# Cross-attention kernel: a third buffer for the exponentials, and new issue orders for TensorE, ScalarE and VectorE

## The reference

```python
qn = _layer_norm(Q, ln_q_g, ln_q_b)
q = (qn @ Wq + bq).reshape(B, Lq, H, DH).transpose(0, 2, 1, 3)
k = (KV @ Wk + bk).reshape(B, Lkv, H, DH).transpose(0, 2, 1, 3)
v = (KV @ Wv + bv).reshape(B, Lkv, H, DH).transpose(0, 2, 1, 3)
scores = jnp.einsum('bhqd,bhkd->bhqk', q, k) / jnp.sqrt(jnp.float32(DH))
attn = jax.nn.softmax(scores, axis=-1)
ctx = jnp.einsum('bhqk,bhkd->bhqd', attn, v)
ctx = ctx.transpose(0, 2, 1, 3).reshape(B, Lq, D)
x = Q + (ctx @ Wo + bo)
h = _layer_norm(x, ln_ff_g, ln_ff_b)
ff = jax.nn.silu(h @ W1 + b1) @ W2 + b2
return x + ff
```

## Time and profile before

| | |
|---|---|
| median of 3 runs | 3438.5 us (3438.05 to 3440.09) |
| the profiled execution's own time | 3438.9 us |
| its span | 3437.1 us |
| TensorE busy | 3363.7 us, 98% |
| VectorE busy | 2505.0 us, 73% |
| ScalarE busy | 2240.1 us, 65% |
| GpSimd busy | 952.1 us, 28% |

### The profile page before, as it was taken

One profiled execution on the slowest core, in us unless ns is written; L12 is line 12 of the kernel. 1 busy time (PEld: TensorE's weight loads), 2 busy tenths in 40 slices (PEclk: granted clock), 3 DMA queues, 4 the chain that ended last, 5 costly groups with the idle time before them and its releaser, 6 DMA issues.

```text
span 3437.1 us, 52453 instructions
## 1 busy us (share of the span) xinstructions
PE 3363.7 (98%) x19620; PEld 1621.4 (47%) x19620; DVE 2505.0 (73%) x4613; ACT 2240.1 (65%) x2859; POOL 952.1 (28%) x1340
## 2 busy tenths in 40 slices
PE   6899999999999999999999999999999999999997
PEld 2334544444444445444445444444444455444435
DVE  5777777777777867777777777767777777777761
ACT  2566667666676666667666676666767666676663
POOL 5032324223332322324222232232314222242201
PEclk7999999999999999999999999999999999999998
DMA  4322212232122322212232122321223231122200
GB/s 103 64 42 44 51 33 55 45 71 42 35 48 36 71 45 43 50 37 57 45 69 38 32 54 38 70 45 35 51 39 61 45 64 36 35 55 43 45 7 13
DMA packets 121534, 162.95 MB, mean 47 GB/s; under 512 B 37040, under 2 KB 102592, under 8 KB 118208
## 3 DMA queue, kind: packets, MB, share of 16 engines
q1 hardware_dynamic: 120896, 159.40, 23.6%
q10 hardware_dynamic: 384, 0.20, 0.0%
HBM read 46.43 MB, written 8.39 MB: 16 GB/s over the span
## 4 chain that ended last, share of the span: by engine, by line
PE 95%; DVE 2%; ACT 1%; SPq 0%; DMA 0%; issue 0%; POOL 0%; ACTq 0%; DVEq 0%
PE o_ps L1241 23%; PE rows_ps L1207 22%; PE scores L1222 21%; PE side L1171 6%; PE side L1175 6%; PE side L1160 5%; PE side L1152 5%; DVE chunk_max L1006 2%; PE side L1156 2%; PE side L1164 2%; PE side L1143 1%; PE side L1146 0%; ACT probs L811 0%; PE scores L1171 0%; PE side L1167 0%; PE side L1150 0%
## 5 line engine op out<-in xcount | busy, mean ns | idle before, releaser
L1006 DVE TENSOR_REDUCE chunk_max<-rows_ps 128x1 f32<-128x512 f32 (+1 forms) x3328 | 2110.8, 666 | 778.7 <-PE rows_ps L1207 772.0
L811 ACT ACTIVATE probs<-scores 128x1024 f32<-128x1024 f32 (+1 forms) x1664 | 1653.4, 1022 | 727.8 <-PE scores L1222 559.7
L1207 PE MATMUL rows_ps<-k_stack,q_stack 96*128 96x512 bf16 (+1 forms) x4096 | 1139.5, 337 | 22.6 <-DVE chunk_max L1006 15.9
L1222 PE MATMUL scores<-q_stack,k_stack 99*128 99x512 bf16 (+1 forms) x3328 | 984.9, 379 | 5.0 <-ACT probs L811 3.0
L1241 PE MATMUL o_ps<-probs,v_sb 128*32 128x512 f32 x6656 | 850.2, 602 | 2.3 <-ACT probs L811 2.2
L1207 PEld LDWEIGHTS rows_ps<-k_stack,q_stack 96*128 96x128 bf16 x4096 | 338.3, 98 | 717.7 <-DVE chunk_max L1006 469.7
L1222 PEld LDWEIGHTS scores<-q_stack,k_stack 99*128 99x128 bf16 (+1 forms) x3328 | 320.0, 99 | 391.1 <-issue 94.5
L1241 PEld LDWEIGHTS o_ps<-probs,v_sb 128*32 128x32 f32 x6656 | 148.9, 108 | 359.8 <-issue 280.9
L648 POOL TENSOR_TENSOR o_sb<-o_sb,denom 128x512 f32<-128x512 f32 x32 | 40.6, 1268 | 896.5 <-DVE denom L992 896.5
L592 POOL TENSOR_TENSOR rest<-whole,k_parts 128x512 f32<-128x512 f32 x124 | 117.1, 944 | 548.7 <-ACT k_parts L776 541.8
L1175 PE MATMUL side<-w_sb,ffT 128*128 128x256 f32 x960 | 261.3, 381 | 0.0
(11 more groups left out here) (130 smaller groups left out, 2160.0 us busy)
## 6 DMA issues: line engine op xcount, KB each, us to landing
k_stack<-k_parts SPq DMA_DIRECT2D x768, 50.0 KB, 2.2
k_stack<-k_stack SPq DMA_DIRECT2D x192, 200.1 KB, 5.6
ctx_nat<-in_ctx SPq DMA_DIRECT2D x47, 512.0 KB, 4.0
q_stack<-q_stack SPq DMA_DIRECT2D x192, 64.0 KB, 3.4
q_stack<-q_parts SPq DMA_DIRECT2D x756, 16.0 KB, 1.8
x_nat<-in_x SPq DMA_DIRECT2D x16, 512.0 KB, 6.0
resid<-in_x SPq DMA_DIRECT2D x32, 256.0 KB, 2.8
out<-resid SPq DMA_DIRECT2D x32, 256.0 KB, 2.4
```

The source lines that it names most:

```text
L811: nc.scalar.activation(probs[0:rows, (q + t) % 2, 2 * LQ * pair:2 * LQ * (pair + 1)], scores[0:rows, 2 * LQ * pair:2 * LQ * (pair + 1)], A ...
L1006: nc.vector.tensor_reduce(dst, src, AX.X, ALU.max).then_inc(rows_read, 1)
L1207: last = nc.tensor.matmul(rows_ps[:, m % 2, d0:d0 + w], q_stack[s][0:STACK, h, P * t:P * (t + 1)], k_stack[s][0:STACK, h, k0:k0 + w], star ...
L1222: ins = nc.tensor.matmul(scores[0:keys_in(t), LQ * j:LQ * (j + 1)], k_stack[s][:, h, P * t:P * t + keys_in(t)], q_stack[s][:, h, :], start ...
```

## The change

`probs` gets three buffers instead of two; tile t of a quarter uses the buffer of its running number over the whole kernel, modulo 3, and the first `e` of a tile waits for the PV of the tile three before. The orders are made anew, with the same letters in the same numbers in every quarter of every string. In TENSOR letters `p` now stand together in twos and threes more often.

```diff
 QT = LQ // P
 HH = H // 2
 UNITS = KT * 2
+PROBS = 3
 PARTS = 3
 K_ROWS = (0, 0, 0, 1, 1, 2)
 Q_ROWS = (0, 1, 2, 0, 1, 0)
...
 
 
 TENSOR = (
-    "pmddsssmmsddddddmssmpmdsssdmdsmddsdddmmpssmmsddmdmdssspmmsddddmddssddmpmmdssssmdmpmmssssmddddmpmsmds"
-    "mdmssddmsmppmsmdssmdmssmdmdmssmsspdmmssdddmssssmddddmppmmddsssmsdmdmpmm",
-    "sspmddmddssmsmddddsmssmpmddddmssssmddddmpssssmmddddmmssssmddmddppmddddmssmssmdpdmmssdmssmdsmmppmmdsm"
-    "dsmmsssdmdssmmpddmmssssddddmmpmddddmssssmmddppmddddmssssmdmddmdmssssmdmdddmmp",
-    "psmmsssddmmddsmdsdmmddssssmmppmdsmsddssmmdddddmssssmmddddppmdmddddddmdsmsssmddddmmpmdddmssmdssdmddms"
-    "dmsssmpmmsspsmmsssdmdmsddmmpsddmsmspssmssmddssmmpdsdddmmpmdmsssmdmpmmss",
-    "dssmmpmsssmsdmmpmsddssmsmdddmmdpmmssssdmmdmssmssmppmssmdssmmssdmdmsdssmmppmmsdsmdmsdmssmddmssmddmdmp"
-    "pmmdssssdmmddssmddmssspddmmspmsssdsdmddmpmssmssmpmm",
+    "pmmddssdmmssdddddmmssssdddddmmssdddmpmmssssdmdmdsmdssmmspppmmddsdsmssmdddmddmssmssmddmssmddddppmmddm"
+    "sssmdmdsmssmpmsssmdmsdmdmdsmsssmppmdssmssmdddmmssssmddddpmmddmdmssdmmpp",
+    "pssmmssmddddmssmssmddddpssmmddddpsmddddmsssmddmssdmdmssssmmddddppmddddmssssmdpdmmssdmmdssssmmddmssmp"
+    "mmdsssmsdmmppmddmssssdddmdmpmddddmssssmmddmmppdmsdddmsssmddmsmsddmdmdsmsddmmp",
+    "pmmsssddmmsddmssmddmddmsssmdddmsssmddmdddmssmssddddmmpppmmsdsdddmmddddssmsmddmdmdsssmmppmmddssmsmsdd"
+    "dmsmsdddmpmmssssddmmddsssmmppmddsmsmdssdsmssmpppddmddssmssmdmmssssmdmmp",
+    "pmmssssmdssmmdssssmmppmmddsssmdmsdmssmddsmmpmsmddmmssssmdmddmdmssssmmpppmmdddmmssdsmdmdssmsmddmssmpm"
+    "ssmdsmdmsssmdmdmppssmssddmsmddsssmmdpmsmdddsssmpmmp",
 )
 SCALAR = (
-    "ceereeereeeereereereeeeeereeerreeeer",
-    "ecrereereereerreererreeerereerererereerreeee",
-    "ceeeeeeerererereeereeeeereereerereere",
-    "eceerreereeereeeereeeeeeeeeeereee",
+    "ceereereeeeeeererreeeeeeereeeerreeer",
+    "ceerereerreeererererreereereeerrerereerreeee",
+    "eceeeeerreeerereeeeereerereeeerreeeer",
+    "ceeeeerreeerereereeeeeeeeeeeeeree",
 )
 VECTOR = (
-    "mmmimimmmmmmmmmmabmmbbmmmmmmmmmmmmmmammbmmmmmmmmnmmgmbmmbgmmmmmmmg",
-    "mmmmmmimmmmxmmxmmimmxmmmmmmmmmmmmmmmmmmmmmmmmgnmmmmmmmmmmmmy",
-    "mmmmmmmimymmmmmmmmimmmmmmmmmmmmmmmmmmmmgmmmmnmmmmmmmmmmgmm",
-    "mmmmmmmmmmmmmimmmmmimmmmmmgmmgmmmmmmmmymmmmmmnmmmymmmmmmmmm",
+    "mmimmmmimmmmmmmmambmbbmmmmmmmmmmmmmmmammmmmmmmmnmmmgmmmbmmmmbgbmmg",
+    "mmmmmmxmmxmmxmmmmmmiimmmmmmmgmmmmmmmmmmmmmmmmmnmmmmmmmmmmmmy",
+    "mmmmmmmymmmmmmmiimmmmmmmmmmmmmmmmmmmgmmmmmmgmnmmmmmmmmmmmm",
+    "mmmimmmmmmmmmmmmgmmmmmmmmigmmmmmmmmmmmymmmmmmnmmmmmymmmmmmm",
 )
 
 
...
         neg_parts = sb("neg_parts", [P, QT, P // 4, 4], BF16)
         shift_parts = sb("shift_parts", [PARTS * 4, LQ], BF16)
         ident_bf = sb("ident_bf", [P, P], BF16)
-        probs = sb("probs", [P, 2, 4 * LQ])
+        probs = sb("probs", [P, PROBS, 4 * LQ])
         o_sb = sb("o_sb", [P, LQ])
         denom = sb("denom", [P, LQ])
 
...
 
             return b * (4 * n) + (n * q + more)
 
+        def probs_of(b, q, t):
+
+            return per_quarter(KT, b, q, t) % PROBS
+
         def walk(eng, prologue, quarter, epilogue, tallies=()):
 
 
...
                 act.wait_ge(scores_ready, per_quarter(UNITS, b, q, u + 1))
                 if pair == 0:
 
-                    wait(act, pv_done, per_quarter(KT, b, q, t - 1))
-                nc.scalar.activation(probs[0:rows, (q + t) % 2, 2 * LQ * pair:2 * LQ * (pair + 1)],
+                    wait(act, pv_done, per_quarter(KT, b, q, t + 1 - PROBS))
+                nc.scalar.activation(probs[0:rows, probs_of(b, q, t), 2 * LQ * pair:2 * LQ * (pair + 1)],
                                      scores[0:rows, 2 * LQ * pair:2 * LQ * (pair + 1)], ACT.Exp)\
                     .then_inc(exp_done, 1)
 
...
                 for j in range(4):
                     col = VH * (4 * (q % 2) + j) - DH * (q % 2)
                     last = nc.tensor.matmul(o_ps[32 * j:32 * j + 32, :], v_sb[q // 2][0:rows, t, col:col + 32],
-                                            probs[0:rows, (q + t) % 2, LQ * j:LQ * (j + 1)],
+                                            probs[0:rows, probs_of(b, q, t), LQ * j:LQ * (j + 1)],
                                             start=(t == 0), stop=(t == KT - 1))
                 last.then_inc(pv_done, 1)
```

## The result

The changed kernel takes 3388.95 us (median of 4, 3388.29 to 3390.71) against 3439.02 us for the kernel before in the same measurement (median of 4, 3438.05 to 3440.09): a ratio of 0.9855, 95% interval 0.9838 to 0.9872. The profiled execution took 3389.6 us.

A forecast was written before the change was run, and what follows sets the result against it. TensorE's own steps, end to end, were taken to bound the full batches. From the profiled 3438.9 us, 38.6 us for merged PV runs and 0 us for new waits gave 3400.3 us, as median 3400 us; range 3391 to 3413 us.

The forecast's parts named there:

- Steps 1 and 2: On TensorE, putting two PV runs together saves 0.23 us; a full batch goes from 41 runs to 30.
- Step 3: Merges bring 36.5 us in full batches and the last batch's first quarter, 2.1 us in other edge quarters: 38.6 us.
- Step 4: In a run of three PVs on TensorE, the middle tile costs 0.86 us, like a second tile, not 1.09 us.
- Step 5: In the full batches, the new orders add 0 us of waits on TensorE; upper bound 0.7 us after a triple.
- waits that swallow the merges: After each of 81 triples TensorE waits 0.7 us for ScalarE or VectorE, 57 us in all: 3457 us; chance 0.04.
- waits that come back: Some TensorE waits return once or twice per batch, 0.8 us on average, 12 us in all: 3412 us; chance 0.17.
- a dear middle tile: A middle tile of a triple costs as much as one alone, 18.6 us less gained: 3419 us; chance 0.04.
- The edges gain more: First and last batch gain more, as the third buffer also removes waits for exponentials there: 3392 us; chance 0.09.

## Why the forecast was right in sign and too small

- Steps 1 and 2, the price of a run and their number: right. Split triples gave 1.27 us for five runs, with some 0.05 us of wait in it; one merge gave its 0.231 us and 0.106 for a load uncovered no more. The 30 runs of a full batch after are 13 single, 12 double and 5 triple, not 15, 11 and 5, which would be 31; the sum goes by the 30.
- Step 3, what they bring: right. 11 x 0.231 = 2.54 us of the 3.23 us per full batch. The first and last batch gave 3.6 us where 3.0 were put; no run shows how much of this the merges are.
- Step 4, the middle tile: right. The triple goes from 1256.84 to the turn of the maxima at 1259.56, which is 2.72 us as worked out, not 2.95, and the loads in its middle are covered:

```profile
1256.84 2.78 PE L1246 MATMUL o_ps<-probs,v_sb 128*32 128x512 f32 x24
1257.30 0.13 PEld L1246 LDWEIGHTS o_ps<-probs,v_sb 128*32 128x32 f32 x4 [0.30 <-ACT probs L816]
1257.73 0.13 PEld L1246 LDWEIGHTS o_ps<-probs,v_sb 128*32 128x32 f32 x4 [0.30 <-issue]
...
1259.56 0.23 PE L1151 MATMUL side<-ident_bf,neg_parts 128*128 128x128 bf16 x1
```

- Step 5, no new waits in the full batches: right but for two waits for a transfer by the starts, 0.3 us at some 348 and 0.75 us at some 1368 us. Its other half was never asked. I took the full batch for "TensorE's own steps, end to end" on the strength of 0.5 us in the list of waits and a busy share of 100%, and so asked only which waits the new orders could add, not which they could remove. **This is the step that failed.** The batch held 0.33 us of hidden waits and 0.53 us of uncovered weight loads. By the starts, after, 0.04 and 0.32 us of these are left: 0.50 of the 0.69 us beyond the merges. The other 0.19 us lie in steps that differ by 0.05 us or less each, and no run isolates them. Times 14, the 0.50 us are 7.0 us; all of the 0.69 us, less the 1.1 us of the two waits, is the 8.6 us.
- The other missing term is the closing stretch, 2.9 us in the profiled executions. It goes with the granted clock, and neither the new orders nor the third buffer is needed for it: with before's orders it took 52.6 us with three buffers and 53.2 to 53.7 us with two, against 55.5. What makes the clock differ there stays open. The opening took back 1.5 us, at a mean granted clock of 0.77 instead of 0.80; no run isolates it.
- Of the rivals, waits that swallow the merges, waits that come back and a dear middle tile did not occur. "The edges gain more" had the right size of time, 3392 us, by the wrong place: the first and last batch gave 3.6 us, and waits for exponentials there hardly changed (5.6% of the last batch's chain after, 6.1% before).
- That two buffers would not do for the triples is an argument and was not tried: the exponentials of a run's third tile must be finished before its first PV has freed a buffer.

## What to carry to other kernels

Before calling a stretch "one engine end to end", subtract start from start for every step and compare equal steps with their cheapest case: a wait that is shorter than a record's overlap with the next one (here 0.16 us) counts as busy, and so does a load behind an unusual neighbour. A change of order should then be costed with what it removes of these as well as what it adds, over every engine's order and every transfer, since an operation that meets its DMA too early holds all behind it. Where VectorE and GpSimd both work on SBUF, look at who runs beside whom, not only at how long each is busy.

## What the runs showed of the hardware

- VectorE's scalar_tensor_tensor of 128 x 512 took 1.37 us instead of 0.68 where it overlapped a GpSimd addition of 1.27 us, and even one of 128 x 128 took 0.98 us.
- A float32 side product of 128 weight columns costs 0.08 us more behind four short products of 65 columns and 0.11 us more behind a PV with its 32-column weights than behind a score or a full maxima product.
- Merging PVs is worth 0.231 us per run and a tile within a run costs 0.86 us, in doubles and triples alike. The Trainium skill (TensorE: Matmul & The Clock Gate, What overlaps and what doesn't) lets weight loads overlap only across row groups; the loads inside these runs, all on the same rows, are covered, so the measurement decides against it here.
- The thin closing stretch took 55.5 us in one execution and 52.6 us in another with the same instructions, at a mean granted clock of 0.82 and 0.87, and 52.5 to 53.7 us in the nine other kernels profiled.
